# Where TensorE passes over the version of its program that isn't run: behind the attention stage, or behind the last matrix product

## The reference

```python
mod = silu(c) @ wmod                        # -> sa, ca, ga, sb, cb, gb, each (8, 1, 1024)
ga, gb = clamp(ga), clamp(gb)               # sign kept, size at least 0.25
h = layernorm(x) * (1 + ca) + sa
attn = (w1 @ w2.T) * sparse_mask            # (1024, 1024)
x = x + ga * gelu(h^T-mix by attn + b2)     # einsum('bds,st->bdt', h, attn)
h = layernorm(x) * (1 + cb) + sb
H = (h @ U1) @ V1 + b1                      # rank 256, 2 * 2752 columns
x = x + gb * ((silu(gate) * up) @ U2 @ V2 + b2)
```

## Time and profile before

| | us |
|---|---|
| median of 3 runs | 1187.37 |
| lowest and highest | 1185.20, 1188.64 |
| the profiled execution | 1187.63 |
| its span, first to last instruction | 1185.8 |
| PE busy (share of the span) | 1148.8 (97%) |
| DVE, ACT, POOL busy | 586.5, 490.3, 391.6 |
| PE instructions recorded (matrix products) | 5882 |

### The profile page before, as it was taken

The page is one execution under the profiler, slowest core; times in us unless marked ns, Lnnn a source line. Parts: engine busy times, 40 slices in busy tenths (PEclk is TensorE's granted clock), DMA queues, the critical chain, the costliest instruction groups (busy, mean ns, idle before and its releaser), DMA issues.

```text
span 1185.8 us, 15387 instructions
## 1 busy us (share of the span) xinstructions
PE 1148.8 (97%) x5882; PEld 952.3 (80%) x5882; DVE 586.5 (49%) x940; ACT 490.3 (41%) x789; POOL 391.6 (33%) x339
## 2 busy tenths in 40 slices
PE   5798899998999999999999999999999999999998
PEld 5577788897888788888888888888888888888886
DVE  3456687785765334434434343443443434444343
ACT  2136567676887543223224323323322432332341
POOL 1008889891113657313031130211303113021110
PEclk9898999999999999999999999999999999999999
DMA  9993998857654542511130150131113015013101
GB/s 361 387 345 109 321 349 307 305 189 258 237 213 178 166 138 78 187 55 71 54 125 27 45 177 1 72 113 65 71 53 126 17 56 178 1 72 105 37 1 71
DMA packets 57484, 169.59 MB, mean 143 GB/s; under 512 B 6208, under 2 KB 11072, under 8 KB 55360
## 3 DMA queue, kind: packets, MB, share of 16 engines
q1 hardware_dynamic: 57408, 168.57, 39.8%
HBM read 126.51 MB, written 42.04 MB: 142 GB/s over the span
## 4 chain that ended last, share of the span: by engine, by line
PE 83%; DMA 5%; POOL 4%; DVE 3%; SPq 2%; issue 1%; ACT 1%; DVEq 0%; POOLq 0%; ACTq 0%
PE bank L546 22%; PE bank L548 22%; PE bank L547 22%; PE bank L722 4%; PE bank L609 3%; PE bank L923 2%; PE bank L930 2%; PE bank L925 2%; DMA wm_sb<-in_wmod 2%; POOL g L1584 2%; POOL xs L1587 1%; PE bank L583 1%; SPq L378 1%; DMA x_dram<-xs 1%; DVE bn L1223 1%
## 5 line engine op out<-in xcount | busy, mean ns | idle before, releaser
L1156 ACT ACTIVATE act<-bank,b_sb 128x512 f32<-128x512 f32 (+1 forms) x176 | 121.3, 690 | 497.3 <-PE bank L548 481.4
L1499 DVE SCALAR_TENSOR_TENSOR act<-bank,b_sb,act 128x512 f32<-128x512 f32 (+1 forms) x176 | 132.0, 750 | 376.5 <-PE bank L548 353.4
L546 PE MATMUL bank<-pt,v_hi 128*128 128x512 f32 x688 | 268.6, 390 | 0.0
L547 PE MATMUL bank<-pt,v_hi 128*128 128x512 f32 x688 | 267.7, 389 | 0.0
L548 PE MATMUL bank<-pt,v_lo 128*128 128x512 f32 x688 | 267.6, 389 | 0.0
L1654 POOL TENSOR_TENSOR x2t<-gbb_bc,x2t 128x512 f32<-128x512 f32 x64 | 86.1, 1368 | 245.3 <-DMA x2t<-x_dram 245.3
L1509 DVE TENSOR_TENSOR act_lo<-act,act_hi 128x512 fp32r<-128x512 f32 (+1 forms) x176 | 160.3, 911 | 0.8
L546 PEld LDWEIGHTS bank<-pt,v_hi 128*128 128x128 f32 x688 | 129.1, 188 | 29.3 <-DVE act L1499 2.6
L548 PEld LDWEIGHTS bank<-pt,v_lo 128*128 128x128 f32 x688 | 129.1, 188 | 27.1
L547 PEld LDWEIGHTS bank<-pt,v_hi 128*128 128x128 f32 x688 | 129.1, 188 | 26.7
L546 PE MATMUL bank<-act_hi,u_hi 128*128 128x512 f32 x336 | 131.0, 390 | 0.8 <-DVE act_lo L1509 0.7
(11 more groups left out here) (134 smaller groups left out, 1670.6 us busy)
## 6 DMA issues: line engine op xcount, KB each, us to landing
xs<-in_x SPq DMA_DIRECT2D x32, 512.0 KB, 5.6
wm_sb<-in_wmod SPq DMA_DIRECT2D x8, 2048.0 KB, 10.2
x_dram<-xs SPq DMA_DIRECT2D x32, 512.0 KB, 5.1
xs<-x_dram SPq DMA_DIRECT2D x32, 512.0 KB, 5.4
x2t<-x_dram SPq DMA_DIRECT2D x32, 512.0 KB, 4.1
out<-x2t SPq DMA_DIRECT2D x31, 512.0 KB, 4.9
pt_dram<-pt_st SPq DMA_DIRECT2D x8, 1024.0 KB, 4.4
pt<-pt_dram SPq DMA_DIRECT2D x8, 1024.0 KB, 5.7
```

Of the source, the lines that this page charges most:

```text
L546: nc.tensor.matmul(acc, s_hi, m_hi, start=start, stop=False)
L547: nc.tensor.matmul(acc, s_hi, m_lo, start=False, stop=False)
L1156: nc.scalar.activation(act[0:w, j % 2, :], bank[0:w, j % 2, :], ACT.Silu, bias=b1_sb[0:w, i, 0:1]).then_inc(silu_done, 1)
L1499: nc.vector.scalar_tensor_tensor(act[0:w, j % 2, :], up, b1_sb[0:w, i, 1:2], act[0:w, j % 2, :], ALU.add, ALU.mult).then_inc(act_done, 1)
```

## The change

The low-rank loop and the feed-forward of TensorE become functions, and both `If` blocks call all three stages. No instruction that runs is added or taken away apart from branches, and the code of the other engines is the same.

```diff
-            with nc.tensor.If(dense == 0):
-                first_batch(False)
-                for b in range(1, NB):
-                    attention(b, False)
-            with nc.tensor.If(dense != 0):
-                first_batch(True)
-                for b in range(1, NB):
-                    attention(b, True)
-
-            for b in range(NB):
-                t = NB + b
...
+            def low_rank():
+                for b in range(NB):
+                    t = NB + b
...
+            def feed_forward():
+                pe.wait_ge(pt_lo_ready, 2 * NB - 2)
...
+            def whole_program(whole):
+                first_batch(whole)
+                for b in range(1, NB):
+                    attention(b, whole)
+                low_rank()
+                feed_forward()
+
+            with nc.tensor.If(dense == 0):
+                whole_program(False)
+            with nc.tensor.If(dense != 0):
+                whole_program(True)
```

More of the change, by code:

```diff
@@ L821, in attention @@
                 y(b, 7, whole)
-            with nc.tensor.If(dense == 0):
-                first_batch(False)
-                for b in range(1, NB):
-                    attention(b, False)
-            with nc.tensor.If(dense != 0):
-                first_batch(True)
-                for b in range(1, NB):
-                    attention(b, True)
-            for b in range(NB):
-                t = NB + b
[L834 to L842, removed]
+            def low_rank():
+                for b in range(NB):
+                    t = NB + b
+                    for k in range(4):
+                        turn(t, 4 + k)
+                        p_product(b, k)
+                        if b == 0 and k == 0:
+                            beta2_turn()
+                    for k in range(4):
+                        if b < NB - 1:
+                            turn(t + 1, k)
+                        p_product(b, 4 + k)
             def h_waits(b, q, j):
@@ L945, in batch @@
                 out_product(b)
[L948 to L958, removed]
+            def feed_forward():
+                pe.wait_ge(pt_lo_ready, 2 * NB - 2)
+                for i in range(2):
+                    gate_product(0, 0, i)
+                    if i == 1:
+                        pe.wait_ge(pt_lo_ready, 2 * NB)
+                    up_product(0, 0, i)
+                batch(0, 0, False)
+                for i in range(1, NB // 2):
+                    batch(i * 2 - 1, 1, False)
+                    batch(i * 2, 0, False)
+                batch(NB - 1, 1, True)
+            def whole_program(whole):
[8 more added lines that the diff above has]
+                whole_program(True)
         @block.scalar
```

## The result

| | before | changed |
|---|---|---|
| median | 1187.43 us (20 runs) | 1189.14 us (20 runs) |
| lowest and highest | 1184.66, 1189.52 | 1187.30, 1194.62 |
| ratio, 95% interval | | 1.0018 [1.0009, 1.0026] |
| profiled execution | 1187.63 | 1188.72 |
| span | 1185.8 | 1186.9 |

The changed kernel is 0.18% slower, 1.7 us at the median. That is within the 0.3% I called "no change", and inside the range, but its interval excludes 1.

What follows compares the result with a forecast made beforehand. The prediction took TensorE, busy 97% of the span, as the bound. 1187.63 us plus 0 for seam, clock and end gave 1187.6, forecast as 1187.4 since that execution was 0.26 above the median; range 1184.7 to 1190.2.

Steps and rivals of the forecast that it cites:

- no change: Whole kernel: differences within 0.3%, 3.6 us (1183.8 to 1190.9), count as the same; chance of same 0.89.
- The seam is worth nothing: Between attention and low-rank loop: the 1.21 us branch stall goes, but TensorE waits longer at L665; gain 0.
- The clock: TensorE's half-speed stretch behind the L665 wait: stays 3.41 us long, change 0; bounds kept were -1.7 and +1.5 us.
- The end costs nothing: Behind TensorE's last product: the branch is hidden by the last tile's addition and store, 3.4 us of room; cost 0.
- the second rival: Behind the last product: a second fetch, or the closing waiting for TensorE, adds up to 2.2 us, 1189.6; chance 0.08.
- The sum: Whole kernel: profiled 1187.63 plus 0 (seam), 0 (clock), 0 (end) gives 1187.6; forecast as a time 1187.4 us.

Runs made afterwards that it cites:

- b1: Kernel before, with beta2_turn (L665) moved behind the third of the low-rank loop's products instead of the first: 1186.17 us, ratio 0.9992.
- b2: Changed kernel, with beta2_turn (L665) moved behind the third of the low-rank loop's products instead of the first: 1186.77 us, ratio 0.9988.
- b4: Changed kernel, with beta2_turn behind the third low-rank product and the skipped dense != 0 version between low-rank loop and feed-forward: 1184.85 us, ratio 0.9976.
- e1: Changed kernel without the dense != 0 version in TensorE's program, so no branch and nothing to pass over: 1188.90 us, ratio 1.0005.
- e3: Changed kernel with TensorE waiting, ahead of the branch at the end, until all stores have landed: 1191.55 us, ratio 1.0032.
- e4: Changed kernel with the skipped dense != 0 version moved between the low-rank loop and the feed-forward: 1187.95 us, ratio 1.0005.
- e5: Changed kernel with the dense != 0 version standing twice at the end, so two are passed over in turn: 1192.39 us, ratio 1.0032.
- after_again: The changed kernel once more, unaltered, in a second set of 11 runs: 1188.73 us, ratio 1.0004 to the kernel before.
- e2: Kernel before with a third If (dense != 0) behind its last product, holding the whole other version: 1187.68 us, ratio 1.0004.

## Why the prediction was right or wrong

- **The seam is worth nothing: right.** L708 to L665 is 6.15 or 6.16 us in eight profiles, with and without the pass-over. With the wait at L665 filled, the pass-over costs 1.4 us (b1 against b2 to b4).
- **The clock: right in size, with luck in it.** In five executions with the one gap of 3.9 us (e1, e3, e4, e5 and after_again) the low clock began 0.0 to 0.3 us after L665 and lasted 3.41 us. In the sixth, the changed kernel's first, it began inside the gap and lasted 6.83. The forecast gave no reason for the same length but the equal sum of idle time. The excess of 0.75 us (910.65 against 909.90 in the same kernel) is within the +1.5 that I kept as a bound.
- **The end costs nothing: wrong, and this is the step that failed.** I asked only when TensorE arrives, and the bound held: at worst 3.0 us after the start of its last product, measured 2.79. (The likelier figure, 1.21 us behind the end of the last product, did not: it took that stall for the length of a pass-over.) I then held against the second rival that at the end the transfer engines carry little, so that a fetch should be no slower. I didn't ask what the fetch does to the transfers. Those engines carry the last stores, on which the span ends, and aren't idle: their share is 0.91 in the first microsecond of the end (the row at 1182.04 above). One packet of code takes 0.93 us of one engine, and the stores' rows on that engine stand behind it. The term "end" was 1.2 us (4.99 and 4.93 against 3.75) and not 0. e1 and e3 against the changed kernel show the cause: 2.72 us to the last store without the packet, 4.25 with it. The 1.53 us between them are more than the packet's 0.93; the rest I put down to the time before the packet's start in which one engine carries no stores. Why it stands idle there is open.
- **The second rival, "the end shows", had the right place and sign** (a chance of 0.08) and the wrong mechanism: no second fetch before TensorE closes, and no wait for TensorE. The end waits for TensorE only where the branch stands behind the stores (e3) or two pass-overs follow each other (e5). That the total came out so near the forecast is because the missing term is small against 1187 us, not because every term was right.
- **The sum.** 1.2 us at the end and 0.3 to 0.4 between L665 and the last product (909.80 to 909.90 in the executions of e3, e5 and after_again, 909.51 in e1, e2 and e4) make 1.5 to 1.6, against 1.7 measured by 20 runs (0.0009 to 0.0026 of 1187.4 is 1.1 to 3.1 us). The 11 runs of after_again gave 0.5 us (-0.7 to 1.5), which agrees in the upper part only. What the 0.3 are is open. They lie in the low-rank loop, whose step takes 1.833 us instead of 1.827 in those executions. e3, e5 and the changed kernel have their code where e1 has it, which doesn't show it, so the addresses are hardly the reason, and no experiment was aimed at it.

## What to carry to other kernels

Passing over a long piece of code costs what the branch's 3.4 to 4.3 us stick out of the work already issued: next to nothing behind 16 products that take 3.6 us and more, 1.2 to 1.6 us behind 16 short ones, all of it where the engine stands still. Don't put it behind the last product, however idle the engine is there, because the fetch travels on the same transfer engines as the last stores (1.2 us here); and before moving a stall, look at what waits next and fill that first, since here it was the moved `beta2_turn` that made the placing of the branch worth anything.

## What the runs showed of the hardware that I had not expected

- One block of code (0.02 MB) moves as a single packet on one transfer engine, for 0.93 us alone (e3), 0.93 to 1.9 us beside the last stores, and 1.65 and 2.46 us when two are under way (e5). A store spread over all sixteen engines is as late as that one engine: here by 1.2 us.
- A compare-and-branch took 0.08 us where the code that runs stands next, and 3.36 to 4.35 us where it passes over a whole version (5.01 for the second of two in e5). Except for that second one, 1.35 to 1.52 us of it lie behind the end of its packet each time.
- TensorE reached the branch 16 products ahead, at the seam as in e4_mid: 1.95 us before the start of the last of them there and 3.8 here. At the end of the kernel before, its closing instruction is recorded 1.54 us before the last product starts.
- The kernels' same products reach L708 at times 3.6 us apart in twelve profiles (264.95 to 268.52), while L708 to the last product differs by 1.15 us at most among the first eight kernels of the table. So most of the profiles' spread comes from in front of the seam. The low clock differs there too: 3 to 5 falls, of 3.41 or 6.83 us each. No experiment was aimed at it.
